# Relative attention: values in column strips, mask in the fused maximum, score blocks of two heads alternating

## The chip, the cores and the metric

The kernel runs on one core of a Trainium2 chip. The time is device microseconds from start to end of one execution; lower is better. Engines are named TensorE (PE in the profile, PEld its weight loads), VectorE (DVE), ScalarE (ACT), GpSimd (POOL) and SyncE (SP). TensorE's clock is granted at one of two levels, 1.2 or 2.4 GHz; the profile gives it as a share of the full one.

## The reference, cut to what matters

The input is 8 sequences of 512 tokens with 128 features. Each goes through eight residual layers: attention, mixture of experts, attention, mixture of experts, linear attention, adapter, relative attention, adapter, with a layer norm before each. The change touches only the relative attention (16 heads of 8 features, n = 512, d = 128):

```python
srel = srel_skew(jnp.einsum('bhnd,hmd->bhnm', qx, ex))
qk = (jnp.einsum('bhnd,bhmd->bhnm', qx, kx) + srel) * inv_dim
mask = 1000000000.0 * jnp.triu(jnp.ones((n, n), dtype=x.dtype), 1)
atten = jax.nn.softmax(qk - mask, axis=-1)
out = jnp.einsum('bhnm,bhmd->bhnd', atten, vx).transpose(0, 2, 1, 3).reshape(b, n, d)
return out @ Wp.T + bp
```

## The kernel before

A loop of eight turns does one sequence each, layer after layer; every engine has its own program, and semaphores order them. Tokens are four tiles of 128 (`NT`), and only the ten tile pairs on and below the diagonal (`BLOCKS`) are computed.

In the relative attention the relative term is first written to `sc`, for all heads and the ten blocks, key on the partition axis. Then comes the loop over the 16 heads, the stage that the change touches. It is software-pipelined: turn `i` of it starts head `i`, has head `i-1` in its row maxima and exponentials, head `i-2` in its transposes, and head `i-3` in its values.

- `qk(h, j)`: a head's score products, bf16 with three-part splits stacked on 48 partitions (`stacked`; odd heads begin at partition 64), in three jobs: 512 columns (key tile 0), 512 (key tiles 1 and 3), 256 (key tile 2). After each product of a key tile, a product `identb x mask_kq` adds the mask to its diagonal block. The jobs alternate between PSUM banks 0 and 1.
- VectorE's `add(h, j)` adds the bank to `sc`.
- `rows(h)`: ten transposes of `sc` into banks 2, 3 and 4, so that the query is on the partition axis (`ROW_JOBS`: query tiles 3, 2, 0 and 1).
- VectorE's `row_max(h)` takes the negated maximum of each query tile from the bank; ScalarE's `exps(h)` reads the bank, subtracts the maximum, and writes the exponentials to `r_prob`, which has two buffers by `h % 2`. `exps(h)` waits on `r_pT` until the transposes of head `h-2` have read the buffer.
- `columns(h, j)`: ten transposes of `r_prob` back to key on the partition axis, in three jobs that alternate between banks 5 and 6. ScalarE copies the first two jobs, VectorE (`column`) the third, to `r_probT`.
- `weigh(h)` calls `weigh_columns`: four products of the head's nine value columns (eight and a one for the sum) with `r_probT`, into 32 partitions of bank 7. An fp32 product is two instructions on TensorE, so that a head has eight value pieces.
- When a group of four heads is done, ScalarE copies bank 7 (`group_columns`), TensorE transposes it (`group_rows`), and VectorE's `heads_out` divides by the sum.

The other two attention layers (`pe_attn`) already compute their values with `weigh_group`, four heads in four 32-column strips of the array, and their row maxima with the fused instruction that adds `mask_row` (L1369).

Of the kernel before, what the change touches and what calls it, by code (L numbers as in the profile page):

```python
# [35 lines left out]
H = 16  # L36
# [38 lines left out]
def build(nc, a_x, a_wq, a_wk, a_wv, a_wo, b_wattn, b_wout, m_ws, m_bs, m_wg, m_wu, m_wd,  # L75
# [10 lines left out]
    with ExitStack() as ctx:  # L86
# [104 lines left out]
        r_probT, at2 = part(ring_at + 2 * COLS, [2, COLS])  # L191
        sc, at = part(at2, [H, len(BLOCKS), P])
        r_neg_max, at = part(at, [2, NT])
        r_rden, at = part(at, [2, NT, G4])

# [112 lines left out]
        r_pTa = sem("rel_prob_columns_act")  # L308
        r_pTv = sem("rel_prob_columns_vec")
# [59 lines left out]
        ROW_JOBS = [(3, 2, 0), (2, 3, 0), (0, 3, 3 * P), (1, 4, 0)]  # L369
# [245 lines left out]
        def group_columns(eng, n, G, bk):  # L615

            if n == 2:
                eng.wait_ge(a_pv, G4 * (G + 1))
# [95 lines left out]
        def act_rel(eng):  # L714
# [19 lines left out]
            def exps(h):  # L734
                at = {0: 0, 1: P, 2: 3 * P, 3: 6 * P}
                if h >= 2:
                    eng.wait_ge(r_pT, 3 * (h - 1))
                for n, (t, bk, col) in enumerate(ROW_JOBS):
                    eng.wait_ge(r_max, 4 * h + (3 if n == 1 else n + 1))
                    eng.activation(r_prob[:, h % 2, at[t]:at[t] + (t + 1) * P],  # L740
                                   bank(bk)[:, col:col + (t + 1) * P], ACT.Exp,
                                   bias=r_neg_max[:, h % 2, t:t + 1]).then_inc(r_p, 1)

            def columns(h):
                for j in range(2):
                    eng.wait_ge(r_pT, 3 * h + j + 1)
                    if h >= 2:
                        eng.wait_ge(a_pv, h - 1)
                    eng.activation(r_probT[:, h % 2, JOB_AT[j]:JOB_AT[j] + JOB_N[j]],  # L749
                                   bank(5 + (3 * h + j) % 2)[:, 0:JOB_N[j]], ACT.Copy).then_inc(r_pTa, 1)  # L750

            for i in range(1, H + 3):
                if i - 3 >= G4 and (i - 3) % G4 == 0:
                    group_columns(eng, 2, (i - 3) // G4 - 1, 7)
                if 2 <= i <= H + 1:
                    columns(i - 2)
                if i <= H:
                    exps(i - 1)
# [60 lines left out]

        def weigh_columns(eng, bk, h, p_cols):  # L820

            row = 32 * (h % G4)
            for s in range(NT):
                at = P * SLOT[(s, s)]
                m = eng.matmul(bank(bk)[row:row + HD + 1, P * s:T], values[:, s, h, :],  # L825
                               p_cols[:, h % 2, at:at + T - P * s], start=(s == 0), stop=(s == NT - 1))
            m.then_inc(a_pv, 1)
# [299 lines left out]
        def pe_rel(eng, w):  # L1127
# [26 lines left out]
            def qk(h, j):  # L1154
                k = 3 * h + j
                if k >= 2:
                    eng.wait_ge(r_sum, k - 1)
# [7 lines left out]
                for s in JOBS[j]:  # L1165
                    N = T - P * s
                    eng.matmul(bank(k % 2)[:, col:col + N], stacked(k_st, h, slice(P * s, P * s + P)),  # L1167
                               stacked(q_st, h, slice(P * s, T)), start=True, stop=False)
                    m = eng.matmul(bank(k % 2)[:, col:col + P], identb[:, :], mask_kq[:, :],  # L1169
                                   start=False, stop=True)  # L1170
# [3 lines left out]
            def rows(h):  # L1174
                eng.wait_ge(r_sum, 3 * (h + 1))
                for i, (t, bk, col) in enumerate(ROW_JOBS):
                    if h >= 1 and i != 2:
                        eng.wait_ge(r_p, 4 * (h - 1) + (1, 3, 3, 4)[i])
# [3 lines left out]
                    if i != 1:  # L1182
                        m.then_inc(r_sT, 1)

            def columns(h, j):
                at = {0: 0, 1: P, 2: 3 * P, 3: 6 * P}
                k = 3 * h + j
                if j == 0:
                    eng.wait_ge(r_p, 4 * (h + 1))
                    if h >= G4 + 2 and h % G4 == 2:  # L1190
                        eng.wait_ge(a_o, 2 * NG + h // G4)
                if k >= 2:
                    h2, j2 = (k - 2) // 3, (k - 2) % 3
                    if j2 < 2:
                        eng.wait_ge(r_pTa, 2 * h2 + j2 + 1)
                    else:
                        eng.wait_ge(r_pTv, h2 + 1)
                first = JOB_AT[j] // P
                for b in range(first, first + JOB_N[j] // P):
                    s, t = BLOCKS[b]  # L1200
                    m = eng.transpose(bank(5 + k % 2)[:, P * (b - first):P * (b - first) + P],  # L1201
                                      r_prob[:, h % 2, at[t] + P * s:at[t] + P * s + P], ident[:, :])
                m.then_inc(r_pT, 1)

            def weigh(h):
                G, hh = h // G4, h % G4
                eng.wait_ge(r_pTa, 2 * h + 2)
                eng.wait_ge(r_pTv, h + 1)
                if hh == 0 and G >= 1:
                    eng.wait_ge(a_cols, 2 * NG + G)  # L1210
                weigh_columns(eng, 7, h, r_probT)

            for i in range(H + 3):
                if i < H:
                    qk(i, 0)
                    qk(i, 1)
                if 1 <= i <= H:
                    rows(i - 1)
                if 2 <= i <= H + 1:
                    columns(i - 2, 0)  # L1220
                    columns(i - 2, 1)
                if i < H:
                    qk(i, 2)
                if 2 <= i <= H + 1:
                    columns(i - 2, 2)
                if i - 3 >= G4 and (i - 3) % G4 == 0:

                    eng.wait_ge(r_pTa, 2 * (i - 2) + 2)
                    group_rows(eng, 2, (i - 3) // G4 - 1, 5 + (3 * (i - 2) + 1) % 2)
                if i >= 3:  # L1230
                    weigh(i - 3)
# [35 lines left out]
        def _(eng):  # L1267
# [295 lines left out]
            def rel():  # L1563
# [30 lines left out]
                def add(h, j):  # L1594
                    k = 3 * h + j
                    eng.wait_ge(r_main, k + 1)
                    b = JOB_AT[j] // P
                    v = sc[:, h, b:b + JOB_N[j] // P, :].rearrange("p b i -> p (b i)")
                    eng.tensor_tensor(v, v, bank(k % 2)[:, 0:JOB_N[j]], ALU.add).then_inc(r_sum, 1)  # L1599

                def row_max(h):
                    for i, (t, bk, col) in enumerate(ROW_JOBS):
                        eng.wait_ge(r_sT, 3 * h + (1, 2, 2, 3)[i])
                        eng.tensor_reduce(r_neg_max[:, h % 2, t:t + 1], bank(bk)[:, col:col + (t + 1) * P], AX.X,  # L1604
                                          ALU.max, negate=True).then_inc(r_max, 1)
# [103 lines left out]
```

## Time and profile before

| what | value |
|---|---|
| median of 3 runs | 4981.29 us (4979.67, 4981.29, 5001.24) |
| profiled execution: time | 4969.21 us |
| profiled execution: span, first to last instruction | 4967.5 us |
| mean granted clock of TensorE | 0.912 |
| TensorE busy | 4473.0 us (90%) |
| VectorE, ScalarE, GpSimd busy | 2379.6, 1719.1, 843.7 us |
| first turn of the head loop of the relative attention | 516.7 to 622.8 us |

The profile is that of one execution. Busy time is the union of an engine's instructions; the loop of the relative attention comes eight times, once in each turn.

### The profile page before, as it was taken

The numbers are of one execution on the slowest core, as the hardware profiler recorded it, in microseconds if no ns is written. First come the engines' busy times: TensorE is split into PE (matmuls) and PEld (weight loads), VectorE is DVE, ScalarE is ACT, GpSimd is POOL, SyncE is SP. The second block draws the span as 40 slices with busy tenths as digits, with TensorE's granted clock in tenths as the row PEclk, the third lists the DMA queues.
The fourth block names the chain that finished last, engine by engine and source line by source line (L and its number), as shares of the span: only waits on it lengthen the run. The fifth ranks groups of instructions, "written<-read, shape, count | busy, mean of one in ns | idle before, by whom it ended". The sixth has DMA issues, their size and how long they took to land.

```text
span 4967.5 us, 76834 instructions
## 1 busy us (share of the span) xinstructions
PE 4473.0 (90%) x30219; PEld 2776.4 (56%) x30275; DVE 2379.6 (48%) x6906; ACT 1719.1 (35%) x3496; POOL 843.7 (17%) x1441
## 2 busy tenths in 40 slices
PE   7998989889898898988989889899898998989989
PEld 3556645565455654556545575455754457545575
DVE  3435634356443554435544355444554445544455
ACT  2322432325333343333433234333343333433334
POOL 2003110031100311103011040111401114011130
PEclk8989979999899998999989999899998999998989
DMA  2000000000000000000000000000000000000000
GB/s 68 1 1 1 1 6 1 1 1 1 6 1 1 1 1 6 1 1 1 1 6 1 1 1 1 6 1 1 2 1 6 1 1 2 1 3 1 1 1 3
DMA packets 19571, 17.25 MB, mean 3 GB/s; under 512 B 2462, under 2 KB 18799, under 8 KB 19183
## 3 DMA queue, kind: packets, MB, share of 16 engines
q1 hardware_dynamic: 19183, 11.99, 0.8%
q8 instruction: 254, 4.16, 0.4%
q14 instruction: 134, 1.10, 0.1%
HBM read 9.89 MB, written 2.10 MB: 2 GB/s over the span
## 4 chain that ended last, share of the span: by engine, by line
PE 80%; DVE 6%; POOL 6%; ACT 5%; issue 3%; DVEq 0%; ACTq 0%; POOLq 0%; SPq 0%
PE banks L984 7%; PE banks L974 7%; PE banks L988 7%; PE banks L880 7%; PE banks L908 6%; PE banks L825 6%; PE banks L920 3%; POOL work L478 3%; PE banks L865 3%; PE banks L1180 3%; PE banks L1201 2%; PE banks L1167 2%; PE banks L1074 2%; PE banks L1047 2%; PE banks L1023 2%
## 5 line engine op out<-in xcount | busy, mean ns | idle before, releaser
L1369 DVE CUSTOM_DVE_ANT_0 work<-banks,mask_row 128x512 f32<-128x512 f32 (+3 forms) x1024 | 451.6, 488 | 274.0 <-PE banks L880 270.6
L880 PE MATMUL banks<-work 32*128 32x512 f32 (+3 forms) x2048 | 526.7, 493 | 11.4 <-DVE work L1369 11.4
L908 PE MATMUL banks<-work 32*128 32x256 f32 (+3 forms) x2048 | 512.7, 504 | 20.8 <-ACT work L638 20.8
L638 ACT ACTIVATE work<-banks 128x384 f32<-128x384 f32 (+1 forms) x768 | 368.9, 526 | 441.9 <-PE banks L908 440.3
L437 POOL TENSOR_TENSOR rstd<-rstd,half 128x2 f32<-128x2 f32 x128 | 87.5, 703 | 2451.2 <-DVE moments L1297 1834.2
L654 ACT ACTIVATE work<-banks 128x512 f32<-128x512 f32 (+1 forms) x384 | 228.8, 596 | 687.6 <-PE banks L984 687.4
L1441 DVE TENSOR_TENSOR work<-work,banks 128x512 f32<-128x512 f32 (+1 forms) x384 | 263.5, 686 | 344.8 <-PE banks L988 344.5
L984 PE MATMUL banks<-xnT,wg 128*128 128x512 f32 (+1 forms) x768 | 417.8, 627 | 0.0
L988 PE MATMUL banks<-xnT,wu 128*128 128x512 f32 (+1 forms) x768 | 406.1, 611 | 0.0
L447 POOL TENSOR_SCALAR_AFFINE_SELECT work<-work 128x128 f32<-128x128 f32 (+1 forms) x768 | 252.6, 332 | 897.4 <-ACT work L638 886.1
L974 PEld LDWEIGHTS banks<-wd,work 128*128 128x128 f32 (+1 forms) x3072 | 360.6, 191 | 57.3 <-issue 57.3
L880 PEld LDWEIGHTS banks<-work 32*128 32x128 f32 x2048 | 259.0, 198 | 216.8 <-DVE work L1369 141.3
L974 PE MATMUL banks<-wd,work 128*128 128x128 f32 (+1 forms) x3072 | 361.0, 274 | 0.0
L1599 DVE TENSOR_TENSOR work<-work,banks 128x512 f32<-128x512 f32 (+1 forms) x384 | 229.2, 599 | 269.6 <-PE banks L1169 238.1
L908 PEld LDWEIGHTS banks<-work 32*128 32x128 f32 x2048 | 252.3, 198 | 125.3 <-ACT work L638 80.0
L825 PE MATMUL banks<-work,values 128*9 128x512 f32 (+3 forms) x1024 | 290.7, 433 | 0.0
L790 PE MATMUL banks<-ident,xn 128*128 128x128 f32 x256 | 85.3, 418 | 215.2 <-DVE xn L1303 212.4
L749 ACT ACTIVATE work<-banks 128x512 f32<-128x512 f32 x256 | 139.1, 595 | 377.3 <-PE banks L1201 377.3
L1426 DVE SCALAR_TENSOR_TENSOR x<-banks,work,x 128x128 f32<-128x128 f32 x512 | 144.2, 344 | 248.3 <-PE banks L974 248.3
L988 PEld LDWEIGHTS banks<-xnT,wu 128*128 128x128 f32 (+1 forms) x768 | 143.8, 187 | 206.1 <-issue 206.1
L740 ACT ACTIVATE work<-banks,work 128x512 f32<-128x512 f32 (+3 forms) x512 | 229.5, 543 | 43.4 <-DVE work L1604 43.4
L1604 DVE TENSOR_REDUCE work<-banks 128x1 f32<-128x512 f32 (+3 forms) x512 | 216.4, 483 | 22.9 <-PE banks L1180 22.9
(255 smaller groups left out, 7254.4 us busy)
## 6 DMA issues: line engine op xcount, KB each, us to landing
x_next<-in_L_attn_a_x_dram SPq DMA_DIRECT2D x8, 256.0 KB, 2.8
out_dram<-x SPq DMA_DIRECT2D x8, 256.0 KB, 2.2
wg<-in_L_ffn_Wg_dram SPq DMA_DIRECT2D x1, 1376.0 KB
wu<-in_L_ffn_Wu_dram SPq DMA_DIRECT2D x1, 1376.0 KB
wd<-in_L_ffn_Wd_dram SPq DMA_DIRECT2D x2, 512.0 KB
wk_l<-in_L_attn_a_Wk_dram SPq DMA_DIRECT2D x1, 512.0 KB, 7.8
wv_l<-in_L_attn_a_Wv_dram SPq DMA_DIRECT2D x1, 512.0 KB, 6.5
wq_l<-in_L_attn_a_Wq_dram SPq DMA_DIRECT2D x1, 512.0 KB, 7.2
```

What stands on the lines that cost most here:

```text
L447: eng.affine_select(out=v, in_=v, compare_op=ALU.is_ge, fill=0.0, base=0, pattern=[[0, 2], [1, P]] if j == 2 else [[1, P]], channel_multip ...
L638: eng.activation(prob4[:, G % 2, hh, C_AT[j]:C_AT[j] + C_N[j]], bank(3 + c % 3)[:, 0:C_N[j]], ACT.Exp).then_inc(s_exp, 1)
L740: eng.activation(r_prob[:, h % 2, at[t]:at[t] + (t + 1) * P], bank(bk)[:, col:col + (t + 1) * P], ACT.Exp, bias=r_neg_max[:, h % 2, t:t + ...
L825: m = eng.matmul(bank(bk)[row:row + HD + 1, P * s:T], values[:, s, h, :], p_cols[:, h % 2, at:at + T - P * s], start=(s == 0), stop=(s == ...
L880: m = eng.matmul(bank(k % 3)[:, col:col + N], q4[own, G, P * t:P * t + P], k4[own, G, 0:N], start=True, stop=True)
L908: m = eng.matmul(bank(3 + c % 3)[:, col:col + N], k4[own, G, P * s:P * s + P], q4[own, G, P * s:T], start=True, stop=True)
L974: m = eng.matmul(bank(4 + e % 2)[:, P * t:P * t + P], hidden[0:w, e % 2, j, P * t:P * t + P], wd[0:w, e, j, :], start=(j == 0), stop=(j == ...
L984: eng.matmul(bank(i % 2)[0:w, :], wg[:, e, f0:f0 + w], xnT[:, :], start=True, stop=True).then_inc(m_g, 1)
L988: eng.matmul(bank(2 + i % 2)[0:w, :], wu[:, e, f0:f0 + w], xnT[:, :], start=True, stop=True).then_inc(m_u, 1)
L1369: m = eng.tensor_tensor_reduce(out=summed[:, k % 2, col:col + N], in0=bank(k % 3)[:, col:col + N], in1=mask_row[:, T - N:T], scale=1.0, sc ...
L1441: eng.tensor_tensor(hidden[0:w, e % 2, j, :], silu[0:w, i % 2, :], bank(2 + i % 2)[0:w, :], ALU.mult).then_inc(m_h, 1)
L1599: eng.tensor_tensor(v, v, bank(k % 2)[:, 0:JOB_N[j]], ALU.add).then_inc(r_sum, 1)
```

## The change

1. The heads go in pairs (`PAIRS` = 8). `qk(p, j)` issues the blocks of the pair's two heads alternately, one head to bank 0, the other to bank 1, and waits until both additions of the job before are done. The mask products are gone.
2. VectorE's `row_max(h, jobs)` is the fused instruction: it adds `mask_row`, writes the masked scores to `r_prob` and the maximum to `r_top`; one `tensor_scalar` per head negates the four maxima into `r_neg_max` (semaphore `r_neg`). Its first job waits on `r_pT` for the transposes of head `h-2`. `exps(h)` works in place on `r_prob`.
3. ScalarE copies all three jobs of `columns(h)`, into the head's own blocks of `sc`; `r_probT` and VectorE's `column` are gone.
4. `weigh(G)` does a group of four heads at once, in four column strips, 32 instructions.
5. `ROW_JOBS` puts query tiles 0 and 1 both in bank 4, and the order within an iteration is written anew on TensorE, VectorE and ScalarE.

The core of the diff:

```diff
+        ROW_JOBS = [(3, 2, 0), (2, 3, 0), (0, 4, 2 * P), (1, 4, 0)]
+        PAIRS = H // 2
...
             def exps(h):
+                eng.wait_ge(r_neg, h + 1)
+                for t, _, _ in ROW_JOBS:
+                    v = r_prob[:, h % 2, ROW_AT[t]:ROW_AT[t] + (t + 1) * P]
+                    eng.activation(v, v, ACT.Exp, bias=r_neg_max[:, h % 2, t:t + 1]).then_inc(r_p, 1)
 
             def columns(h):
+                own = sc[:, h, :, :].rearrange("p b i -> p (b i)")
+                for j in range(3):
                     eng.wait_ge(r_pT, 3 * h + j + 1)
+                    eng.activation(own[:, JOB_AT[j]:JOB_AT[j] + JOB_N[j]],
                                    bank(5 + (3 * h + j) % 2)[:, 0:JOB_N[j]], ACT.Copy).then_inc(r_pTa, 1)
 
+            for i in range(1, PAIRS + 2):
+                if i >= 2:
+                    exps(2 * i - 3)
+                    columns(2 * i - 4)
+                if i <= PAIRS:
+                    exps(2 * i - 2)
+                if i >= 2:
+                    columns(2 * i - 3)
+                if i >= 4 and i % 2 == 0:
+                    group_columns(eng, 2, i // 2 - 2, 7)
...
+            def qk(p, j):
+
+                k = 3 * p + j
+                if k >= 1:
+                    eng.wait_ge(r_sum, 2 * k)
...
+                    for r in range(2):
+                        m = eng.matmul(bank(r)[:, col:col + N], stacked(k_st, 2 * p + r, slice(P * s, P * s + P)),
+                                       stacked(q_st, 2 * p + r, slice(P * s, T)), start=True, stop=True)
...
+            def columns(h):
+                for j in range(3):
+                    k = 3 * h + j
+                    if j == 0:
+                        eng.wait_ge(r_p, 4 * (h + 1))
+                    if k >= 2:
+                        eng.wait_ge(r_pTa, k - 1)
...
+            def weigh(G):
+
+                eng.wait_ge(r_pTa, 3 * G4 * (G + 1))
+                if G >= 1:
+                    eng.wait_ge(a_o, 2 * NG + G)
+                for s in range(NT):
+                    at = SLOT[(s, s)]
+                    for hh in range(G4):
+                        h = G4 * G + hh
+                        m = eng.matmul(bank(7)[32 * hh:32 * hh + 32, P * s:T],
+                                       val_row[:, s, BELOW * h:BELOW * h + 32],
+                                       sc[:, h, at:at + NT - s, :].rearrange("p b i -> p (b i)"),
+                                       start=(s == 0), stop=(s == NT - 1))
+                m.then_inc(a_pv, 1)
+
+            for i in range(PAIRS + 2):
+                if i < PAIRS:
+                    qk(i, 0)
+                if i >= 5 and i % 2 == 1:
+                    group_rows(eng, 2, (i - 5) // 2, 7)
+                if 1 <= i <= PAIRS:
+                    rows(2 * i - 2)
+                if i < PAIRS:
+                    qk(i, 1)
+                if i >= 2:
+                    columns(2 * i - 4)
+                if 1 <= i <= PAIRS:
+                    rows(2 * i - 1)
+                if i < PAIRS:
+                    qk(i, 2)
+                if i >= 4 and i % 2 == 0:
+                    weigh(i // 2 - 2)
+                if i >= 2:
+                    columns(2 * i - 3)
+            weigh(NG - 1)
...
+                def add(p, j):
+                    eng.wait_ge(r_main, 3 * p + j + 1)
                     b = JOB_AT[j] // P
+                    for r in range(2):
+                        v = sc[:, 2 * p + r, b:b + JOB_N[j] // P, :].rearrange("p b i -> p (b i)")
+                        eng.tensor_tensor(v, v, bank(r)[:, 0:JOB_N[j]], ALU.add).then_inc(r_sum, 1)
+
+                def row_max(h, jobs):
+
+                    for i in jobs:
+                        t, bk, col = ROW_JOBS[i]
+                        N = (t + 1) * P
+                        eng.wait_ge(r_sT, 3 * h + (1, 2, 3, 3)[i])
+                        if h >= 2 and i == 0:
+                            eng.wait_ge(r_pT, 3 * (h - 1))
+                        eng.tensor_tensor_reduce(out=r_prob[:, h % 2, ROW_AT[t]:ROW_AT[t] + N],
+                                                 in0=bank(bk)[:, col:col + N], in1=mask_row[:, T - N:T],
+                                                 scale=1.0, scalar=MASKED, op0=ALU.add, op1=ALU.max,
+                                                 accum_out=r_top[:, h % 2, t:t + 1]).then_inc(r_max, 1)
+                    if jobs[-1] == 3:
+                        eng.wait_ge(r_max, 4 * (h + 1))
+                        eng.tensor_scalar(r_neg_max[:, h % 2, :], r_top[:, h % 2, :], -1.0, None,
+                                          ALU.mult).then_inc(r_neg, 1)
+
+                for i in range(PAIRS + 2):
+                    if i < PAIRS:
                         add(i, 0)
+                    if 1 <= i <= PAIRS:
+                        row_max(2 * i - 2, (0, 1, 2, 3))
+                    if i >= 5 and i % 2 == 1:
+                        heads_out(2, (i - 5) // 2, 7, r_rden)
+                    if i < PAIRS:
                         add(i, 1)
+                    if 1 <= i <= PAIRS:
+                        row_max(2 * i - 1, (0, 1))
+                    if i < PAIRS:
+                        add(i, 2)
+                    if 1 <= i <= PAIRS:
+                        row_max(2 * i - 1, (2, 3))
```

## Rows read from the trace of the kernel before

**Rows 1.** The page: the chain that ended last, share of the span by engine.

```profile
PE 80%; DVE 6%; POOL 6%; ACT 5%; issue 3%; DVEq 0%; ACTq 0%; POOLq 0%; SPq 0%
```

**Rows 2.** Windows: the head loop of turn 1; length, busy per engine, clock, DMA.

```profile
516.70:622.80 106.10, 104.45 (x588) 59.37 (x588) 61.62 (x134) 47.50 (x101) 1.11 (x3) 0.95 0.00 1
```

**Rows 3.** The chain in order of time, turn 1: start, us, what.

```profile
521.28 2.13 PE banks L1180 x10
...
542.56 0.32 PE banks L1167
542.88 0.16 PE banks L1169
...
543.79 1.10 PE banks L1180 x10
544.88 0.87 PE banks L1201 x8
...
546.45 2.25 PE banks L825 x8
548.70 0.32 PE banks L1167
...
554.84 0.32 PE banks L1167
...
561.69 0.32 PE banks L1167
```

**Rows 4.** Windows around the start and behind the end of the loop; PEclk third from last.

```profile
516.00:520.00 4.00, 2.34 (x10) 0.95 (x10) 1.65 (x3) 1.91 (x4) 1.81 (x4) 0.93 0.00 0
...
519.20:529.60 10.40, 10.24 (x44) 7.00 (x43) 7.12 (x15) 2.49 (x5) 0.00 (x0) 0.51 0.00 0
529.60:534.20 4.60, 4.60 (x34) 3.23 (x34) 3.99 (x9) 3.39 (x8) 0.00 (x0) 0.99 0.00 0
...
628.00:632.00 4.00, 2.12 (x8) 1.36 (x7) 2.33 (x14) 0.00 (x0) 0.63 (x1) 0.58 0.00 0
```

**Rows 5.** The chain in the first attention layer: column strips, projections and values.

```profile
39.62 0.99 PE banks L865 x8
...
86.28 1.00 PE banks L920 x8
...
91.01 0.78 PE banks L920 x8
...
94.71 0.79 PE banks L920 x16
```

**Rows 6.** Timeline of the head loop, turn 1: start, us, engine, line, operation.

```profile
518.04 1.65 DVE L1599 TENSOR_TENSOR work<-work,banks 128x512 f32<-128x512 f32 x3 [2.29 <-PE banks L1169]
...
544.43 1.68 DVE L1604 TENSOR_REDUCE work<-banks 128x1 f32<-128x512 f32 x4
...
544.72 1.04 PE L1201 MATMUL banks<-ident,work 128*128 128x128 f32 x8
545.36 1.09 ACT L749 ACTIVATE work<-banks 128x512 f32<-128x512 f32 x2 [3.38 <-PE banks L1201]
...
546.01 0.44 PE L1201 MATMUL banks<-ident,work 128*128 128x128 f32 x2
...
546.33 1.79 ACT L740 ACTIVATE work<-banks,work 128x512 f32<-128x512 f32 x4
```

**Rows 7.** Groups of instructions by form, VectorE: count, busy, mean ns, idle before.

```profile
L1369 DVE CUSTOM_DVE_ANT_0 work<-banks,mask_row 128x512 f32<-128x512 f32 x256 | 167.9, 688 | 78.5 <-PE banks L880 77.9
...
L1604 DVE TENSOR_REDUCE work<-banks 128x1 f32<-128x512 f32 x128 | 87.7, 685 | 20.5 <-PE banks L1180 20.5
...
L1299 DVE TENSOR_SCALAR rstd<-moments 128x1 f32<-128x1 f32 x256 | 32.0, 145 | 0.0
```

**Rows 8.** Windows elsewhere in turn 1 with TensorE partly idle.

```profile
100.00:104.00 4.00, 2.80 (x35) 1.38 (x33) 0.55 (x2) 1.97 (x5) 1.58 (x4) 1.00 0.00 0
...
480.00:484.00 4.00, 2.99 (x10) 1.26 (x12) 4.00 (x4) 1.08 (x2) 2.03 (x1) 0.74 0.00 0
```

More of the change, by code:

```diff
@@ L190, in build @@
         r_prob, _ = part(ring_at, [2, COLS])
-        r_probT, at2 = part(ring_at + 2 * COLS, [2, COLS])
-        sc, at = part(at2, [H, len(BLOCKS), P])
+        sc, at = part(ring_at + 4 * COLS, [H, len(BLOCKS), P])
         r_neg_max, at = part(at, [2, NT])
         r_rden, at = part(at, [2, NT, G4])
+        r_top, _ = part(ring_at + 2 * COLS, [2, NT])
         silu, at = part(0, [2, T])
@@ L617, in group_columns @@
             if n == 2:
-                eng.wait_ge(a_pv, G4 * (G + 1))
+                eng.wait_ge(a_pv, G + 1)
             else:
@@ L818, in pe_spread @@
                         m.then_inc(a_spread, 1)
[L820 to L827, printed above, removed]
         def group_rows(eng, n, G, bk):
@@ L1174, in rows @@
             def rows(h):
-                eng.wait_ge(r_sum, 3 * (h + 1))
+                eng.wait_ge(r_sum, 6 * (h // 2 + 1))
                 for i, (t, bk, col) in enumerate(ROW_JOBS):
-                    if h >= 1 and i != 2:
-                        eng.wait_ge(r_p, 4 * (h - 1) + (1, 3, 3, 4)[i])
+                    if h >= 1 and i < 3:
+                        eng.wait_ge(r_max, 4 * (h - 1) + (1, 2, 4)[i])
                     for s in range(t + 1):
@@ L1181, in rows @@
                                           ident[:, :])
-                    if i != 1:
+                    if i != 2:
                         m.then_inc(r_sT, 1)
[L1185 to L1214, printed above, removed]
-                    qk(i, 0)
-                    qk(i, 1)
[L1217 to L1222, printed above, removed]
-                    qk(i, 2)
[L1224 to L1231, printed above, removed]
+            def columns(h):
[5 more added lines that the diff above has]
+                        eng.wait_ge(r_pTa, k - 1)
+                    first = JOB_AT[j] // P
+                    for b in range(first, first + JOB_N[j] // P):
+                        s, t = BLOCKS[b]
+                        m = eng.transpose(bank(5 + k % 2)[:, P * (b - first):P * (b - first) + P],
+                                          r_prob[:, h % 2, ROW_AT[t] + P * s:ROW_AT[t] + P * s + P], ident[:, :])
+                    m.then_inc(r_pT, 1)
@@ L1607, in column @@
-                def column(h):
-                    eng.wait_ge(r_pT, 3 * h + 3)
-                    if h >= 2:
-                        eng.wait_ge(a_pv, h - 1)
-                    eng.tensor_copy(r_probT[:, h % 2, JOB_AT[2]:JOB_AT[2] + JOB_N[2]],
-                                    bank(5 + (3 * h + 2) % 2)[:, 0:JOB_N[2]]).then_inc(r_pTv, 1)
-                for i in range(H + 2):
-                    if i < H:
-                        add(i, 0)
+                    for r in range(2):
+                        v = sc[:, 2 * p + r, b:b + JOB_N[j] // P, :].rearrange("p b i -> p (b i)")
+                        eng.tensor_tensor(v, v, bank(r)[:, 0:JOB_N[j]], ALU.add).then_inc(r_sum, 1)
@@ L1621, in rel @@
                         add(i, 2)
-                    if i >= 2:
-                        column(i - 2)
-                    if i - 3 >= G4 and (i - 3) % G4 == 0:
-                        heads_out(2, (i - 3) // G4 - 1, 5 + (3 * (i - 2) + 1) % 2, r_rden)
+                    if 1 <= i <= PAIRS:
+                        row_max(2 * i - 1, (2, 3))
                 heads_out(2, NG - 1, 7, r_rden)
```

46 lines of the change are left out of this document (3 added, 43 removed).

## The prediction

> **What bounds the kernel now.** I read the page first: TensorE holds 80% of the chain that ended last [rows 1]. That is an average over eight layers, and the change touches one stage of one layer, the loop over the 16 heads of the relative attention. So I went to the first of the eight turns and took its windows, its chain and its timeline.
>
> The loop runs from 516.7 us (first score product) to 622.8 us (last copy of a group's values): 106.1 us a turn, TensorE busy 104.45, VectorE 61.62, ScalarE 47.50 [rows 2]. A steady head lasts 6.14 us (542.56 to 548.70), and the chain through it is TensorE alone: ten transposes 1.10, eight of the probabilities 0.87, values 2.25, and 1.92 for score products, masks and the last two transposes [rows 3]. The head in which a group of four ends takes 6.85 us (554.84 to 561.69), so four heads cost 25.3 us. The clock matters too: TensorE was granted the full clock (2.4 GHz) until shortly before 519.2 us, half of it (1.2 GHz) until about 529.6, then full [rows 4]. Ten transposes cost 2.13 us at half clock and 1.10 at full [rows 3].
>
> **The work that changes**, per turn at full clock. (1) The mask products go: 64 times 0.16 us [rows 3] is 10 us. (2) Values: eight pieces, 2.25 us, per head become 32 per four heads in four column strips. The other attention does this: 1.00, 0.78 and 0.79 us for a group's first, second and last two key tiles [rows 5], 2.57 in all against 9.0. Times four groups: minus 25.7 us. (3) Score blocks of the two heads lie in different row halves of the array and alternate. The trace has no such bf16 pair. One head's four score products are 1.92 less the masks (0.64) and two transposes (0.31): 0.97 us. Bounds for a pair: 0.97 side by side, 1.94 one after the other. Nearest are the projections' strips, eight pieces in 0.99 us [rows 5], where eight such one after the other would take over 3. I take 1.1, minus 6.7 us. Sum: minus 42 us a turn, 340 over eight. (4) VectorE's row maximum becomes the fused form with the mask row, 688 against 685 ns for the 512-wide one [rows 7]: nothing. A 128x4 negation per head is new; nearest row 145 ns [rows 7]. (5) The third copy of transposed probabilities (256 wide) moves from VectorE to ScalarE, and ScalarE's exponentials read SBUF; it is busy for 47.50 of 106.1 us [rows 2], and I cost both at nothing, covered by its waits. Without that cover it would be 0.4 us a head, 51 us in all.
>
> By sums VectorE would need some 7.3 us per pair of heads and TensorE about 7, where a pair now takes 12.3 or more. So the order of waits decides.
>
> **The new chain.** The fused maximum writes its masked scores into `r_prob`, which has two buffers. Before, ScalarE waited for the transposes of head h-2 there; now VectorE waits, ahead of all that is queued behind it: the other maxima and the next additions. TensorE issues `columns(2i-4)` only after `qk(i,1)`, which waits for both additions of job 0 (banks 0 and 1 are single now), and `columns(2i-3)` last, after `qk(i,2)` and `weigh`. The engines take turns.
>
> Unit costs [rows 6]: VectorE's three additions (512, 512, 256 wide) last 1.65 us, so 0.61 start to start for the wide one; two wide additions and the way back to TensorE are 1.35. Four maxima last 1.68, with the negation 1.83. A head's `columns`: 0.64 to ScalarE's first copy (544.72 to 545.36), 0.60 the copy, 0.05 back, two transposes 0.44, 0.04 to VectorE: 1.77; the third job shares its bank with the first, so the copy is inside.
>
> A pair, from its first addition: both additions of job 0 and back 1.35; `qk(i,1)` 0.50 (0.42 side by side, 0.83 not); `columns(2i-4)` 1.77; maxima 1.83; additions of job 1 and back 1.35; `qk(i,2)` 0.25; `columns(2i-3)` 1.77; two maxima 1.09; additions of job 2, the other two maxima and the negation 1.44. Sum 11.35 us, of which TensorE is busy about 5.5. Every odd pair adds `heads_out` on VectorE, 0.5 (at most the 0.71 that it costs a head now [rows 3]); every even one adds the values, 2.5, because `weigh` stands ahead of `columns(2i-3)`. Four heads: 22.7 + 0.5 + 2.5 = 25.7 us. Now they take 25.3. At full clock the whole saving turns into waiting.
>
> Whole loop: pairs 0 and 1, with little to wait for, 11.3; pairs 2 to 7 68.1, two `weigh` 5.0, two `heads_out` 1.0. Tail: 0.5, `rows(14)` 1.1, `columns(12)` 1.77, maxima 1.83, the rest of `rows(15)` 0.4, `weigh(2)` 2.5, `columns(13)` 1.77, maxima of head 15 1.83, its exponentials 1.8 [rows 6], then six copies of heads 14 and 15 with their transposes 3.4, `weigh(3)` 2.6: 19.5. Sum 104.9 against 106.1: minus 1.2 a turn, minus 10 in all. Should the score blocks not overlap, a pair is 0.5 longer, plus 4 us a turn.
>
> **The clock.** It fell in 516 to 520 us, with TensorE busy for 2.34 of 4.00, and in 628 to 632, with 2.12 [rows 4]; with 2.80 (100 to 104) it held [rows 8]. The new loop has 5.5 of 11.35, 1.94 of 4. The dense stretches (`rows`, `columns`, `weigh` before `columns`) lengthen at half clock and should raise it again, as the full stretch from 519.2 did [rows 4]. Price of half clock, per pair: `columns` about 0.65 longer, twice (a transpose 0.21 instead of 0.11); `rows(2i-2)` 2.13, now later than the additions and holding `qk(i,1)` by 0.8; products 0.3: 2.4 us; an odd pair 3.2 (four more transposes), an even one 4.7 (`weigh` doubles). Six pairs 20.6, start-up and tail about 8.4: 29 us a turn if it stayed low, 232 in all. It should alternate, and rise late, in the sparse part; I take 0.45 of that, 13 us a turn. Sum: 8 x (13 - 1.2) = plus 95 us on the profiled 4969, 5064. The median shown stands 12 us above that execution: 5076.
>
> The Trainium skill (TensorE: Matmul & The Clock Gate, PE-mode transpose) says that transposes do not bring the full clock. The new loop is transposes for the most part, so by that rule it would stay at half: rival (b). The trace disagrees: from 519.2 to 529.6 TensorE did only short score products, masks and transposes, and the clock rose [rows 4].
>
> **Rivals.**
> (a) The clock holds at full: 4969 - 10 + 12 = 4971; with unit costs 5% off either way 4930 to 5010. For it: 2.80 of 4 held. Against: the new share is below all that held. 0.17.
> (b) Half clock through the whole loop: 4971 + 232 = 5203. For it: 480 to 484 us, at 2.99 of 4, stood at 0.74 [rows 8]; the new loop at half clock is near 2.9 of 4. 0.12.
> (c) VectorE's wait for `columns` is hidden, and the work's saving comes through: 4969 - 340 + 12 = 4641. It decides where `columns(h-2)` ends before VectorE has done the additions ahead of the maximum; the issue order puts it over 2 us after them. 0.04, with what lies between it and (a) 0.04 more.
> (d) The value strips run one after the other: 9.0 instead of 2.5, four times a turn in the chain: plus 208. Against it: [rows 5]. 0.03.
>
> **Numbers.** The alternating clock has 0.60; its own range is 5000 to 5150 (a share of 0.2 to 0.8). Slower by over 0.5% (about what a measurement of this kernel tells from no change) is over 5006: 0.56 + 0.12 + 0.03 = 0.71. Same, 4956 to 5006: 0.04 + 0.11 = 0.15. Faster: 0.06 of (a) and 0.08 of (c): 0.14. The range, 4955 to 5195, takes in most of (a) and stops short of (b).
>
> **What would show it.** The 512-wide fused maximum in this loop has some 2 us of idle VectorE before it, ended by the probability transposes, twice a pair; TensorE's busy share of the loop falls from 98% to between 50 and 75%; a group's 32 value pieces take 2.3 to 2.6 us at full clock; the granted clock in the loop is 0.65 to 0.85 instead of 0.95; four heads take 26 to 31 us. It is wrong if the fused maximum does not wait there, if the clock holds at such idleness, or if ScalarE's exponentials end so late that the copies wait for them.

## The result and the profile after

| | before | changed |
|---|---|---|
| median | 4980.48 us (4968.94 to 5001.24, 4 runs) | 5089.09 us (5074.42 to 5103.29, 4 runs) |
| profiled execution: time, span | 4969.21, 4967.5 us | 5100.62, 5098.8 us |
| mean granted clock | 0.912 | 0.872 |
| TensorE busy | 4473.0 us | 4326.2 us |

The changed kernel is slower by 2.1% (ratio 1.0213, 95% interval 1.0163 to 1.0263), although TensorE is busy for 147 us less, and that at a lower mean clock. The page's line of the chain that ended last, to be held against [rows 1]:

```profile
PE 72%; DVE 13%; POOL 6%; ACT 6%; issue 3%; DVEq 0%; POOLq 0%; ACTq 0%; SPq 0%
```

The head loop in the windows of turns 1 and 3 of the changed kernel, the counterpart of [rows 2] (busy for TensorE, its weight loads, VectorE, ScalarE, GpSimd; then the clock):

```profile
515.30:628.81 113.51, 75.60 (x524) 49.68 (x524) 56.37 (x198) 56.74 (x116) 1.30 (x3) 0.85 0.00 1
...
1786.47:1902.01 115.54, 77.54 (x524) 51.24 (x524) 56.41 (x198) 56.84 (x116) 1.31 (x3) 0.82 0.00 1
```

TensorE is busy for 75.6 us, many of them at half clock, instead of 104.45, and yet the loop lasts 113.5 us instead of 106. VectorE and ScalarE are busy for half of it. Six of the eight turns take 113.5 us, two 115.5.

The chain of turn 1 (start, us, what; "..." marks what is left out), the counterpart of [rows 3]; L1160 is `qk`, L1171 `rows`, L1186 `columns`, L1199 `weigh`, L1592 the additions, L1602 the fused maximum, L1608 the negation, L746 the copies:

```profile
532.42 1.74 DVE work L1602 x8
...
544.72 1.75 DVE work L1602 x8
546.49 0.17 DVE work L1608
546.66 1.20 DVE work L1592 x2
547.90 0.28 PE banks L1160 x2
548.18 0.60 PE banks L1186 x4
548.81 0.60 ACT work L746
549.46 0.45 PE banks L1186 x2
549.96 0.09 issue
550.04 1.18 DVE work L1602 x4
551.22 0.68 DVE work L1592 x2
551.94 0.61 PE banks L1160 x2
552.55 2.32 PE banks L1171 x10
554.88 0.54 PE banks L1160 x4
555.42 2.38 PE banks L1186 x10
557.85 0.08 issue
557.93 1.74 DVE work L1602 x8
...
561.51 3.75 PE banks L1199 x32
...
573.26 1.75 DVE work L1602 x8
...
589.82 2.29 PE banks L1199 x32
...
612.68 0.71 DVE work L1602 x2
```

One pair of heads goes from one eight-piece maximum to the next. The chain hands over from VectorE to TensorE to ScalarE and back, in the order of the prediction's walk. The granted clock changes within the pair. It is 1.00 from 546.8 to 550.2, and `columns` from 548.18 to 550.04 lasts 1.86 us. From 552.0 to 557.6 it is 0.50: ten transposes of `rows` last 2.32 and `columns` 2.38. From 557.85 to 561.2 it is 0.97, from 561.1 to 565.3 only 0.60, and the values last 3.75 us, where the later group has 2.29. The six steady pairs take 80.3 us (532.42 to 612.68), 26.8 for four heads; they took 25.3.

Who waits for whom, from the groups by form of the changed kernel (busy, mean ns; idle before):

```profile
L1602 DVE CUSTOM_DVE_ANT_0 work<-banks,mask_row 128x512 f32<-128x512 f32 x128 | 88.4, 691 | 370.8 <-PE banks L1186 370.8
```

VectorE idles 370.8 us before the 512-wide maximum, all of it ended by the probability transposes, in 112 of the 128 cases: 14 of 16 heads, 3.3 us each. That is the wait for the buffer of head h-2.

The other layers, whose code is the same, account for a part of the difference between the two profiled executions. From the first transposes of the first norm to those of the second, the first attention layer took 655.4 us over the eight turns before and 705.3 after. Windows of that layer in turns 3 and 2 of the kernel before:

```profile
1277.98:1358.64 80.66, 72.67 (x504) 37.80 (x504) 37.13 (x160) 31.43 (x63) 17.16 (x51) 0.88 0.01 2
654.36:742.51 88.15, 80.75 (x504) 40.94 (x505) 37.40 (x160) 31.69 (x63) 17.15 (x51) 0.79 0.01 2
```

The layer has at least two lengths in the same kernel, 80.66 us at a granted clock of 0.88 and 88.15 at 0.79. Before, one turn in eight had the long one and one 85.3; after, all eight have it (88.1 to 88.2).

The first turn shows that such a difference need not come from the edit. There the layer runs ahead of every edited line, and yet it took 78.1 to 88.2 us over the twelve kernels of this document. Here it is in turn 1 of the kernel before, of "strips alone" and of the changed kernel:

```profile
30.43:111.37 80.94, 72.95 (x504) 38.14 (x505) 37.48 (x160) 31.59 (x63) 17.15 (x51) 0.91 0.03 8
```

```profile
30.39:108.48 78.09, 69.69 (x504) 35.14 (x505) 36.99 (x160) 31.03 (x63) 17.05 (x51) 1.00 0.03 7
```

```profile
30.08:118.30 88.22, 80.83 (x505) 40.95 (x505) 37.40 (x160) 31.68 (x63) 17.07 (x51) 0.79 0.03 7
```

All six layers ahead of the relative attention took 428.1 to 445.8 us in the first turns of the twelve (441.2 in the kernel before, 440.1 in the changed one, whose second attention made up for the first). The change can have had a part only from turn 2 on. There the long length came in 14 turns of 14 in the two kernels with a loop of 113.5 us (the changed one and "heads in turn"), and in one of seven in the kernel before.

Added up over eight turns: loop 844.9 to 912.1 us, plus 67; from the loop's end to the next norm plus 6; first attention plus 50; third layer (the second attention) plus 20; everything else about minus 12. That is the 131 us between the two profiled executions: 73 in the relative attention and 58 outside it. The 58 is of these two executions only. By the medians of four runs each the kernels are 109 us apart, and by the ratio's interval 81 to 131, so if the relative attention brings 73 in each execution, 8 to 58 us are left for the rest (an estimate). The layers outside took 3649 us in the kernel before, the least of the twelve traces, and 3707 in the changed one; the other ten had 3666 to 3713.

### The profile page after: what moved, and what is told of

The parts are those of the page before. It is cut to its first block, busy times and chain, and to the rows that moved or that the text cites. A ratio compares the mean times of both kernels' runs of the same rounds, so it can differ in the third digit from the quotient of the medians.

```text
span 5098.8 us, 76026 instructions
## 1 busy us (share of the span) xinstructions
PE 4326.2 (85%) x29763; PEld 2746.0 (54%) x29763; DVE 2337.9 (46%) x7418; ACT 1795.1 (35%) x3624; POOL 841.7 (17%) x1441
## 4 chain that ended last, share of the span: by engine, by line
PE 72%; DVE 13%; POOL 6%; ACT 6%; issue 3%; DVEq 0%; POOLq 0%; ACTq 0%; SPq 0%
PE banks L871 7%; PE banks L975 7%; PE banks L965 7%; PE banks L979 7%; PE banks L899 6%; PE banks L911 4%; DVE work L1602 4%; POOL work L480 3%; PE banks L1186 3%; PE banks L856 3%; DVE work L1592 3%; PE banks L1065 2%; PE banks L1038 2%; PE banks L1171 2%; PE banks L1199 2%
## 5 line engine op out<-in xcount | busy, mean ns | idle before, releaser
L1362 DVE CUSTOM_DVE_ANT_0 work<-banks,mask_row 128x512 f32<-128x512 f32 (+3 forms) x1024 | 453.1, 488 | 304.9 <-PE banks L871 301.0
L899 PE MATMUL banks<-work 32*128 32x256 f32 (+3 forms) x2048 | 557.9, 555 | 20.8 <-ACT work L640 20.8
L871 PE MATMUL banks<-work 32*128 32x512 f32 (+3 forms) x2048 | 550.0, 522 | 11.4 <-DVE work L1362 11.4
L640 ACT ACTIVATE work<-banks 128x384 f32<-128x384 f32 (+1 forms) x768 | 370.8, 526 | 505.9 <-PE banks L899 503.4
L1434 DVE TENSOR_TENSOR work<-work,banks 128x512 f32<-128x512 f32 (+1 forms) x384 | 263.4, 686 | 341.8 <-PE banks L979 341.7
L871 PEld LDWEIGHTS banks<-work 32*128 32x128 f32 x2048 | 276.4, 211 | 224.4 <-DVE work L1362 141.6
L1602 DVE CUSTOM_DVE_ANT_0 work<-banks,mask_row 128x512 f32<-128x512 f32 (+3 forms) x512 | 225.0, 487 | 370.8 <-PE banks L1186 370.8
L899 PEld LDWEIGHTS banks<-work 32*128 32x128 f32 x2048 | 277.4, 220 | 140.8 <-ACT work L640 77.8
L740 ACT ACTIVATE work<-work 128x512 f32<-128x512 f32 (+3 forms) x512 | 245.6, 550 | 292.0 <-DVE work L1608 292.0
L1171 PE MATMUL banks<-ident,work 128*128 128x128 f32 x1280 | 223.0, 328 | 72.0 <-DVE work L1602 55.6
L790 PE MATMUL banks<-ident,xn 128*128 128x128 f32 x256 | 87.1, 437 | 211.6 <-DVE xn L1296 210.2
L1186 PE MATMUL banks<-ident,work 128*128 128x128 f32 x1280 | 223.0, 316 | 40.8 <-ACT work L746 39.7
L1160 PE MATMUL banks<-work 48*128 48x512 bf16 (+3 forms) x512 | 82.3, 365 | 187.4 <-DVE work L1592 178.8
```

Source lines behind the costliest of these rows:

```text
L640: eng.activation(prob4[:, G % 2, hh, C_AT[j]:C_AT[j] + C_N[j]], bank(3 + c % 3)[:, 0:C_N[j]], ACT.Exp).then_inc(s_exp, 1)
L871: m = eng.matmul(bank(k % 3)[:, col:col + N], q4[own, G, P * t:P * t + P], k4[own, G, 0:N], start=True, stop=True)
L899: m = eng.matmul(bank(3 + c % 3)[:, col:col + N], k4[own, G, P * s:P * s + P], q4[own, G, P * s:T], start=True, stop=True)
L1171: m = eng.transpose(bank(bk)[:, col + P * s:col + P * s + P], sc[:, h, SLOT[(s, t)], :], ident[:, :])
L1362: m = eng.tensor_tensor_reduce(out=summed[:, k % 2, col:col + N], in0=bank(k % 3)[:, col:col + N], in1=mask_row[:, T - N:T], scale=1.0, sc ...
L1434: eng.tensor_tensor(hidden[0:w, e % 2, j, :], silu[0:w, i % 2, :], bank(2 + i % 2)[0:w, :], ALU.mult).then_inc(m_h, 1)
```

## The experiments

Ten more kernels ran, in three sets on three chips, each against the kernel before on the same chip; so the ratios are to be compared, and not the medians. "Loop" is the time from a turn's first score product to the last copy of values, as the typical turn and its mean clock. "Attention 1" is the sum of the first attention layer over eight turns of one profiled execution.

| kernel | median us | ratio (95% interval) | loop, clock | attention 1 |
|---|---|---|---|---|
| before | 4980 | 1 | 105.7, 0.95 | 655 |
| changed | 5089 | 1.0213 (1.0163 to 1.0263) | 113.5, 0.85 | 705 |
| three buffers | 4797 | 0.9648 (0.9617 to 0.9678) | 78.2, 0.93 | 663 |
| values last | 5019 | 1.0084 (1.0047 to 1.0120) | 109.8, 0.83 | 676 |
| strips alone | 4819 | 0.9677 (0.9646 to 0.9709) | 84.0, 0.92 | 679 |
| fused maximum alone | 4958 | 0.9958 (0.9932 to 0.9985) | 98.4, 0.95 | 659 |
| filler | 5074 | 1.0207 (1.0186 to 1.0227) | 110.0, 0.92 | 702 |
| delay before | 4985 | 1.0010 (0.9993 to 1.0026) | 105.7, 0.95 | 675 |
| columns first | 5078 | 1.0214 (1.0190 to 1.0237) | 110.1, 0.85 | 690 |
| three buffers, values last | 4798 | 0.9646 (0.9624 to 0.9668) | 78.1, 0.93 | 671 |
| heads in turn | 5095 | 1.0230 (1.0187 to 1.0273) | 113.5, 0.85 | 698 |
| strips and maximum, old order | 4794 | 0.9612 (0.9585 to 0.9639) | 80.7, 0.89 | 698 |

### Three buffers

```diff
-        r_prob, _ = part(ring_at, [2, COLS])
+        r_prob, _ = part(ring_at, [3, COLS])
...
-                        if h >= 2 and i == 0:
-                            eng.wait_ge(r_pT, 3 * (h - 1))
+                        if h >= 3 and i == 0:
+                            eng.wait_ge(r_pT, 3 * (h - 2))
```

(`r_top` and `r_neg_max` get three as well; all three are indexed by `h % 3`.)

> The changed kernel with three r_prob buffers instead of two (and as many for the maxima), so that the fused maximum of head h waits for the transposes of head h-3. My theory (the two-buffer wait serializes the engines): four heads fall from some 27.5 us to 17 to 19, the head loop from 113.5 us a turn to 75 to 85, the whole kernel to 4750 to 4860 us. Rival 1 (the single score banks, so TensorE's wait for both additions, are what binds): the loop stays above 105 us a turn and the kernel above 5020. Rival 2 (clock alone): the waits remain as long as they are, the granted clock stays at 0.85 and the gain is under 20 us.

Measured: 4797 us, loop 78.2 us, clock 0.93: the theory's numbers. First the window of the loop in turn 2, then what VectorE waited for ahead of the fused maxima (L1602), over all eight turns:

```profile
1110.10:1188.28 78.18, 63.16 (x524) 43.67 (x524) 56.10 (x198) 54.55 (x116) 1.31 (x3) 0.93 0.00 1
```

```profile
its engine sat idle before it (us, times) until:
  PE banks L1171: 21.1, 35
```

The instructions are the same ones; only one wait reaches one head further back. The 370.8 us that ended with `columns` (L1186) are gone. It is worth 35 us a turn, and the clock comes back with it, 0.93 for 0.85. Both rivals fall. The clock alone was not it, since the wait itself went away. The single score banks alone do not hold the loop either: TensorE's idle time before the score products, ended by the additions, went from 395 to 124 us with the banks as they were. Whether a second pair of score banks would have freed the loop as well, with two buffers, no run tested.

### Values last

```diff
-                if i >= 4 and i % 2 == 0:
-                    weigh(i // 2 - 2)
                 if i >= 2:
                     columns(2 * i - 3)
+                if i >= 4 and i % 2 == 0:
+                    weigh(i // 2 - 2)
```

> The changed kernel with only the place of weigh moved: behind columns(2i-3) instead of ahead of it. My theory: the values (2.3 us at full clock, 3.8 where half of them ran at half clock) leave the chain in the three pairs that have them, since VectorE has 2.2 us of maxima and additions to do meanwhile: 7 to 9 us a turn less, the loop at 105 to 107 us instead of 113.5, the kernel 5020 to 5040 us. Rival (weigh is not in the chain, or the next score product then waits for TensorE instead): the loop stays within 2 us of 113.5.

Measured: loop 109.8 us, 3.7 less, half of what was expected, at a clock of 0.83. `weigh` was in the chain. With it gone from there, 31% of the transposes of `columns` ran at half clock instead of 22% (of those of `rows` 34% in both kernels). In the profiled executions the kernel was 74 us below the changed one, but the loop only 34 over eight turns (878.4 against 912.1); the attention layers gave 48 (676 and 641 against 705 and 660), without an edit to them.

### Strips alone, in the kernel before

```diff
-                    eng.activation(r_probT[:, h % 2, JOB_AT[j]:JOB_AT[j] + JOB_N[j]],
+                    eng.activation(sc[:, h, :, :].rearrange("p b i -> p (b i)")[:, JOB_AT[j]:JOB_AT[j] + JOB_N[j]],
...
-                if i >= 3:
-                    weigh(i - 3)
+                if i >= 3 and (i - 3) % G4 == G4 - 1:
+                    weigh((i - 3) // G4)
```

(`weigh(G)` is that of the change; VectorE's copy goes to `sc` too, and the waits for `r_probT` are gone.)

> The kernel before with one part of the change alone: the transposed probabilities are copied into the head's own blocks of the scores, and the values of four heads are computed at once in four column strips; masks, maxima, buffers and order stay. My theory (the strips are a gain by themselves, lost in the change to waiting): minus 25.7 us a turn less at most a third for new waits, so the loop at 80 to 90 us instead of 106, the kernel at 4780 to 4860 us. Rival (the chain through maxima and exponentials takes over at once, near 6 us a head): less than 5 us a turn, the kernel above 4940.

Measured: 4819 us, loop 84.0. The chain where the clock stands at full:

```profile
542.87 0.32 PE banks L1165
...
546.75 0.32 PE banks L1165
...
550.64 2.29 PE banks L1212 x32
552.93 0.32 PE banks L1165
```

A head takes 3.88 us, TensorE all the way, and a group's values 2.29. The strips by themselves are worth 21.7 us of the predicted 25.7 a turn.

### Fused maximum alone, in the kernel before

```diff
-                    m = eng.matmul(bank(k % 2)[:, col:col + P], identb[:, :], mask_kq[:, :],
-                                   start=False, stop=True)
...
+                        if h >= 2 and i == 0:
+                            eng.wait_ge(r_pT, 3 * (h - 1))
...
+                        eng.tensor_tensor_reduce(out=r_prob[:, h % 2, at:at + N],
+                                                 in0=bank(bk)[:, col:col + N], in1=mask_row[:, T - N:T],
```

> The kernel before with the other part alone: no mask products, the mask in the fused maximum, written to r_prob in two buffers, exponentials in place; the order of one head at a time stays, and values are as before. There the transposes of head h-2 stand an iteration ahead of the maximum of head h. My theory: no new wait, minus 64 x 0.16 = 10 us a turn, the loop at 95 to 98 us, the kernel at 4880 to 4920 us. Rival (two r_prob buffers with the maximum as their writer are bad in any order): the fused 512-wide maximum waits for the probability transposes here too, the loop is over 106 us and the kernel over 4985.

Measured: loop 98.4 us in most turns, 7.3 less instead of 10. The same wait on the same two buffers, with VectorE as the writer, costs nothing in the old order: what ended VectorE's idle time before the maxima (L1605) were `rows`' transposes of the scores (L1177), not those of the probabilities.

```profile
its engine sat idle before it (us, times) until:
  PE banks L1177: 23.8, 36
```

The total missed the expectation (4958, not 4880 to 4920): the loop gave 62 us over eight turns (844.9 to 783.1), and the second attention took 46 back (641 to 687).

### Filler

```diff
+            def filler(n):
+                for _ in range(n):
+                    eng.transpose(bank(7)[:, 0:P], ident[:, :], ident[:, :])
```

> The changed kernel with idle TensorE filled: transposes of the identity into the free value bank, 6 behind columns(2i-4) and 7 behind rows(2i-1) in pairs 2, 3, 4 and 6, and 16 behind columns(2i-3) in pairs 2, 3, 5 and 7 (116 a turn; 13 us of TensorE's idle time at full clock). Nothing is removed. Theory (part of the loop's time is half clock that the idling brings): the granted clock in the loop rises from 0.85 to 0.93 or more and the loop gets shorter in spite of more work, from 113.5 to 105 to 109 us. Rival (the clock is not fed by such work, or the loop does not hang on it): clock at most 0.88 and a loop of 113 to 118 us.

Measured: loop 110.0 us in the typical turn at a clock of 0.92 (108.4 at 0.95 in one), against 113.5 at 0.85, with 116 transposes more. So half clock is a part of the loop's time, and with less idle time in TensorE there was less of it: of the transposes of `columns` 1% ran at half clock instead of 22%. Both numbers of the typical turn lie just outside what was expected (0.93 or more, 105 to 109 us). A line through the three points (0.85, 113.5), (0.92, 110.0) and (0.95, 108.4) would meet the full clock at about 106 us, an estimate that stands near the walk's 104.9. The whole kernel did not gain clear of noise: its ratio, 1.0207, is that of the changed kernel. The chain also has one pair wholly at full clock:

```profile
539.12 1.74 DVE work L1614 x8
...
550.54 1.75 DVE work L1614 x8
```

11.42 us; the prediction's walk gave 11.35.

### Delay before

```diff
+                for _ in range(24):
+                    eng.transpose(bank(7)[:, 0:P], ident[:, :], ident[:, :])
                 eng.nop().then_inc(ended, 1)
```

> The kernel before with 24 transposes of the identity at the end of each turn, after the last adapter, which nothing waits for but the turn's end: 2.6 us a turn at full clock, up to 5.1 at half, 21 to 41 us in all. Theory (the change moved 57 us of its 131 profiled into other layers, because the moments at which the clock falls and rises land elsewhere in them): layers whose code is untouched shift by 2 to 8 us in several turns, above all the first attention (78.3, 80.7, 85 or 88.2 us), and the total differs from the direct cost by more than 15 us either way. Rival (the slower first attention comes from the relative attention itself, as through data or buffers): all other layers keep their times within 1 us and the total is plus 21 to 41 us.

Measured: 4985 us, ratio 1.0010 (0.9993 to 1.0026), not clear of none. The profiled span is 17.5 us longer, where the expectation put the direct cost at 21 to 41. That cost was not there at all. The transposes ran while TensorE would have waited for the next turn's norm: at the end of turn 1 its idle time before L790 was 6.83 us before and 4.03 here, and the stretch from the last adapter's norm to the next turn took 176.6 us in eight turns before and 176.8 here. So this run did not delay anything; it filled idle time at the turn's end.

```profile
646.93 2.84 PE L1263 MATMUL banks<-ident 128*128 128x128 f32 x24
...
653.79 1.41 PE L790 MATMUL banks<-ident,xn 128*128 128x128 f32 x4 [4.03 <-DVE xn L1305]
```

The relative attention kept its time (1288.7 us against 1288.4), so nearly all of the 17.5 us lie in layers with untouched code, and the rival's expectation, that all of them stay within 1 us, did not come true. First attention in turns 1, 2 and 4:

```profile
29.97:118.19 88.22, 80.83 (x504) 40.97 (x504) 37.38 (x160) 31.68 (x63) 17.07 (x51) 0.79 0.03 10
653.79:734.44 80.65, 72.67 (x504) 37.71 (x505) 37.11 (x160) 31.48 (x63) 17.07 (x51) 0.88 0.01 3
1882.77:1968.25 85.48, 78.09 (x505) 39.34 (x505) 37.04 (x160) 31.58 (x63) 17.06 (x51) 0.82 0.01 3
```

Before, turn 1 had 80.9, turn 2 88.15 and turn 4 80.66. But turn 1 is over before the first of the added transposes runs, so its 7.3 us came by themselves, and what moved the layer in the later turns this run cannot tell. It shows that the layer moves between its lengths in kernels whose other stages keep their times. That the 58 us outside the relative attention in the changed kernel came by the place at which the loop's end puts the next layers is argued from the clocks and from the 14 turns of 14, and was not isolated.

### Columns first

```diff
+                if i >= 2:
+                    columns(2 * i - 4)
                 if i < PAIRS:
                     qk(i, 1)
-                if i >= 2:
-                    columns(2 * i - 4)
```

> The changed kernel with TensorE's columns(2i-4) ahead of qk(i,1) instead of behind it. By the walk through a pair the fused maximum of head 2i-2 then waits for columns from the end of rows(2i-2) on, not from the additions and qk(i,1): about 1.2 us less a pair, the loop 103 to 107 us instead of 113.5, the kernel 5000 to 5040. Rival (that wait is not in the chain): within 2 us of 113.5. The other wait, at head 2i-1, stays as it is.

Measured: loop 110.1 in four turns and up to 114.2 in the others, so typically 3.4 us less, not 6.5 to 10.5. The additions and `qk(i,1)` did leave the chain; what is there now, ahead of a maximum, is TensorE at half clock:

```profile
550.79 2.33 PE banks L1171 x10
553.11 2.24 PE banks L1186 x10
555.40 0.08 issue
555.49 1.75 DVE work L1602 x8
```

My expectation took full-clock prices for a stretch that stands at half; over the kernel 42% of the transposes of `rows` ran at half clock, 34% in the changed one.

### Three buffers, values last

Both edits from above.

> Three r_prob buffers and weigh behind columns(2i-3), both in the changed kernel. With three buffers the chain runs through ScalarE: exponentials, copies, and the wait of copies for transposes, which weigh holds up by 2.3 us in three pairs. Theory: another 3 to 7 us a turn less than with three buffers alone, loop 71 to 76 us, kernel 4740 to 4790. Rival (VectorE or the score banks bind there): the loop stays at 77 to 79 us.

Measured: 4798 us, loop 78.1, no gain over three buffers alone. The rival's number is right and its reason wrong: the 2.3 us of `weigh` are still there, but have moved. VectorE now waits for the score product issued behind `weigh` (timeline):

```profile
548.93 2.36 PE L1199 MATMUL banks<-work,values 128*32 128x512 f32 x32
...
551.22 0.39 PE L1160 MATMUL banks<-work 48*128 48x512 bf16 x2
...
551.65 1.28 DVE L1592 TENSOR_TENSOR work<-work,banks 128x512 f32<-128x512 f32 x2 [2.47 <-PE banks L1160]
```

The chain goes another way round the same piece: from `weigh` (549.00, 2.33 us) over the copy of the group's values (0.61) and their transposes (0.66) to the next `rows`. ScalarE's exponentials and copies are 20.8 and 15.7% of the chain in 512 to 590 us.

### Heads in turn

```diff
-                for s in JOBS[j]:
-                    N = T - P * s
-                    for r in range(2):
+                for r in range(2):
+                    col = 0
+                    for s in JOBS[j]:
+                        N = T - P * s
```

> The changed kernel with the score blocks of a pair's two heads one head after the other instead of alternating, all else the same. Theory (the row halves work side by side when the blocks alternate, 0.33 us for four pieces of 384, 384, 128 and 128 at full clock): the job of key tiles 1 and 3 takes 0.7 to 0.85 us instead of 0.33 to 0.54, in the chain of a pair 0.4 to 0.8 us more over the three jobs, the loop 3 to 7 us a turn longer, the kernel 5090 to 5160. Rival (the array takes them in turn anyway): the loop within 1 us of 113.5 a turn.

Measured: loop 113.5 us, as in the changed kernel; the rival's number. But its reason, that the array takes the blocks in turn, does not hold. The four pieces of key tiles 1 and 3 last 0.33 us at full clock in either order (here, then in the changed kernel):

```profile
561.87 0.33 PE banks L1161 x4
```

```profile
571.08 0.33 PE banks L1160 x4
```

In the chain of the kernel before, one head's two pieces take 0.27 and 0.16 us, so two heads' one after the other would be 0.86. So the row halves work side by side, and alternating adds nothing to it.

### Strips and maximum in the old order

The edits of strips alone and of fused maximum alone, together in the kernel before.

> The kernel before, one head at a time in its old order, with both useful parts: values in column strips, and the mask in the fused maximum instead of products. TensorE would need 3.9 - 0.54 = 3.4 us a head, VectorE additions 1.57, maxima and negation 1.83 and one copy 0.35 = 3.75 us. Theory (VectorE is the next bound, and two buffers suffice in this order): a steady head 3.7 to 4.0 us, the loop 79 to 84 us a turn against 84 with the strips alone, the kernel 4770 to 4830. Rival (the parts add up, 84 - 8 = 76 us): 74 to 77. Rival 2 (together they bring the turn-taking): over 90.

Measured: 4794 us, loop 80.7 us, inside the theory's range. From 544.52 to 552 VectorE's additions (L1601) and maxima (L1610) hold the chain, but from there to 562 it is TensorE alone, so the theory's reason (VectorE is the next bound) holds for a part of the loop:

```profile
545.12 0.68 DVE work L1601
545.80 1.66 DVE work L1610 x8
...
549.34 0.68 DVE work L1601
550.02 1.66 DVE work L1610 x8
```

This version and three buffers are both faster than the kernel before, by 3.5 to 3.9%, and their intervals overlap.

## Why the prediction was right, and where not

The forecast was 5076 us in 4955 to 5195; measured 5089. The side, the mechanism and the range held. Step by step:

- **What bounds the kernel, what the work costs.** Right. Values 2.29 us a group against 2.57 taken; a strip version without new waits got 21.7 us a turn of 25.7, a mask version 7.3 of 10. So the masks brought a quarter less than their price.
- **The new chain.** Right, and shown: VectorE waits 3.3 us (forecast some 2, at full clock) before the widest fused maximum of 14 of 16 heads for `columns`, and moving that wait back by one buffer alone makes 113.5 us into 78.2. The walk's 11.35 us for a pair at full clock measured 11.42, in "filler".
- **Values in the chain.** Right (values last). But leaving the chain paid only half of what was expected, while `columns` stood at half clock more often.
- **Overlap of the score blocks.** Right that they overlap. The 1.1 us a pair that I took is 1.0 (0.39, 0.33 and 0.28 for the jobs). The alternation that the change is named for is worth nothing.
- **The clock.** Mechanism right, size off. I took 0.45 of 29 us, 13 a turn; a clock of 0.85 is half clock for 0.30 of the loop, and 113.5 less the 104.9 of the walk leaves 8.6. That remainder is all that the walk at full clock lacks; that it is the clock's price fits "filler", which shows the direction, but was not measured by itself. The loop came to 67 us over eight turns, and 6 behind it; forecast was 95.
- **What was missing.** The sum had no term for other layers. They brought 58 us between the two profiled executions, all of it after the first turn. How much of that the change caused stays open, since in the first turns of the twelve kernels the layers ahead of any edit differ by up to 18 us. Against that execution the forecast of 5064 was 37 us short: 22 too many in the loop and behind it, 58 too few outside. So that the median came out 13 us from the forecast is in part luck, two errors of opposite sign.
- **The rule on transposes.** The loop stood at full clock for about 0.70 of its time, though 320 of its 524 TensorE pieces are transposes, and filling idle time with nothing but transposes raised its mean clock from 0.85 to 0.92. The Trainium skill (TensorE: Matmul & The Clock Gate, PE-mode transpose) says that transposes do not bring the full clock; these traces, of fp32 transposes, disagree with it.
- **Rivals.** (a) fell, the clock fell; (b) fell, it came back in each turn; (c) fell in the changed order; three buffers take the wait away, and then 27.5 us a turn of the 42 that (c) counted on come through; (d) fell with 2.29 us a group.

## What to carry to other kernels

When another engine becomes the first writer of a double buffer, follow what is queued behind its wait, and when the reader is issued: the same two buffers with the same writer cost nothing in the old order and 35 us a turn in the order by pairs. Before reordering a stage that leaves TensorE idle for a third of the time, price its dense stretches at half clock, in the chain where they then stand. A change of one stage is to be read by that stage's own time. Layers with untouched code moved the profiled total by 58 us, nearly as much as the loop (67). The first turn, up to the first edited instruction, tells how much such layers move by themselves: here by up to 18 us between kernels.

## What the runs showed of the hardware that I had not expected

- The same attention layer took 78.3, 80.7, 85.4 or 88.2 us with the same instructions, at granted clocks from 0.79 to 1.00, within one kernel and in the first turns of twelve kernels, where no edit has run yet. There it took 88.2 us in the four traces in which it began at 29.8 to 30.1 us, and 78.1 to 85.5 in the eight in which it began at 30.35 to 30.43. So a few tenths of a microsecond in its start may decide; that is a correlation over twelve executions, and no run tests it.
- Score pieces for the two row halves of the array run side by side even when all of one head's come first (0.33 us for four, where one after the other they would take 0.86).
- Four column strips of fp32 values, 32 instructions, last 2.29 us where eight per head took 2.25 for one head.
